# One attention tower on one core: row maxima cut and loaded in two halves, scores three slots later, a fill of one step less

## The chip, the cores and the metric

One Trainium2 chip; the kernel runs on one of its cores. The metric is the time of one execution on the device, in microseconds: before the change, the median of three runs is 1130.84 us (1127.64 to 1141.0). TensorE multiplies matrices into PSUM, VectorE (DVE), ScalarE (ACT) and GpSimd (POOL) compute, and SyncE (SP) issues nearly all DMA transfers, in the order of one list.

## The reference

For 32 sequences of 512 tokens and 128 channels: an embedding, an attention block of 8 heads of 16 channels, and a block of 4 experts, the last two with a residual and a layer norm. What matters here, in short:

```python
h = concat(pos[s], nest[nesting(ids)], seg[segments(ids)]) @ W
q, k, v = split(layernorm(h) @ qkv_w.T + qkv_b)          # 8 heads of 16
attn = softmax(q @ k.T / 4)                              # 512 x 512 per head
h = h + (attn @ v) @ out_w.T + out_b
h = h + experts(layernorm(h))                            # gate, relu(fc1), low rank, fc2
```

All of it is float32.

## The kernel before

Work is staged over sequences. A step t has 16 slots (c = 0 to 15), and in one step each stage works on another sequence: t+4 is embedded, t+3 gets its queries and keys scaled and cut into three bfloat16 pieces, whose stacks (`qstk`, `kstk`) go through DRAM, t+2 and t+1 get row maxima, t gets scores, exponentials and values, t-2 the projection, norm, gate and the first expert product, t-3 the rest. Steps run from -5 to 34, so the first ones fill the pipeline and the last ones empty it.

A head's 512 x 512 scores are made twice. First as 32 maximum tiles per sequence (128 queries x 512 keys, `scores`, L750), two in each slot, whose row maxima VectorE takes (`row_max`, L1025). From slot MSTART = 10 of a step the tiles are those of sequence t+2, before it those of t+1. When all 32 are in, `cut_max` (slot 10 of VectorE) splits the 32 negated maxima of each row into three bfloat16 parts with four chained instructions (L1033 to L1039), TensorE turns them (`turn_max`, L780, slot 11), ScalarE copies the turned rows (`copy_mT`, L610, slot 12), and SP loads them as 24 further rows of `qstk` (`load_max`, L379, "max_in"). Then the score tiles of the next step (`scores_T`, L724, two a slot from slot 0) come out with the maximum already taken off, and ScalarE only takes the exponential (L592). Values (L737) follow in blocks of eight products in slots 7, 11, 15 and 3.

Each engine runs its own written-out list: PE_ORDER and PRODUCTS say what TensorE does in a slot (BEFORE and BEHIND place a product around the values), ACT_WORK and DVE_WORK give (slot, place, name, sequence ahead, part), POOL_WORK and SP_WORK are the order of one step, and POOL_FILL and SP_FILL that of the fill. Maximum tiles and small products share four PSUM banks in turn (`mix`, three uses a slot), so a product may only start when the reader of the use four earlier is done (`mix_free`). Scores have a ring of three banks. Every wait is a semaphore count (`upto`), and an engine stops at it.

`hot` (L996) makes the one-hot of the token ids, `add_qk` (L1010) adds the position part to queries and keys, `finish` (L1104) adds the experts' product to the residual, `invert_den` (L1044) takes the reciprocal of the softmax denominators, and gate_first to gate_fourth (L1055 to L1092) are the chain of the gate. On POOL, `rstd_first` (L460) is a power, `residual`, `second` and `third` (L479, L485, L502) make the pieces, `normalise` (L528, L532) applies the denominators, `value` (L514, L520) writes the values.

## Time and profile before

| what | value |
|---|---|
| median of 3 runs | 1130.84 us (1127.64 to 1141.0) |
| profiled execution | 1126.86 us, its span 1125.1 us |
| TensorE busy | 1040.1 us (92%) |
| VectorE busy | 948.8 us (84%) |
| ScalarE busy | 807.0 us (72%) |
| POOL busy | 682.1 us (61%) |
| mean granted clock of TensorE | 0.962 |
| row maxima (L1025) | 1024 of 679 ns, 649.0 us |
| exponentials (L592) | 1024 of 600 ns, 556.3 us |
| DMA | 132.43 MB, mean 118 GB/s |

Busy times are read per engine from the profile's list. A mean duration of pipelined instructions is longer than the distance between two of them, so a row of several says more than a mean. The rows further down come from one execution; its steps are alike from the third on, and the one that begins at 859.87 us stands for them.

### The profile page before, as it was taken

The page shows a single profiled execution, that of the slowest core. Times are in us where ns is not written, and L with a number is a line of the kernel's source. Part 1 is how long each engine was busy: PE and PEld are TensorE (multiplying, and loading weights), DVE is VectorE, ACT ScalarE, POOL GpSimd, SP SyncE. Part 2 cuts the span into 40 slices and gives each one's busy share as a digit, 9 for nine tenths or more (in the row PEclk, how much of TensorE's full clock was granted, in tenths as well). Part 3 has the DMA queues.
Part 4 walks back from the last instruction along what each step waited for, and adds up shares of the span by engine and source line. Part 5 has one row for each costly group of instructions (what it writes and reads, how often), then busy time and mean ns, then how long its engine had stood idle before and what let it go on. Part 6 is the DMA issues. An engine that isn't in the chain of part 4 may idle for free.

```text
span 1125.1 us, 20263 instructions
## 1 busy us (share of the span) xinstructions
PE 1040.1 (92%) x6158; PEld 407.9 (36%) x6158; DVE 948.8 (84%) x2442; ACT 807.0 (72%) x1578; POOL 682.1 (61%) x684
## 2 busy tenths in 40 slices
PE   4368999999999999999999999999999999989865
PEld 2112233333434434343433443434343343333322
DVE  7498899999989989899999999999999998887312
ACT  2217787777877788787877778778787777856731
POOL 1855676677666666677666666667766666621231
PEclk9558999999999999999999999999999999999997
DMA  2553645555554445555555545565555554541111
GB/s 74 148 135 89 137 106 135 129 137 127 137 130 124 126 121 130 142 127 134 126 137 126 126 121 132 130 143 126 137 125 137 128 126 113 121 96 36 55 50 32
DMA packets 93530, 132.43 MB, mean 118 GB/s; under 512 B 18205, under 2 KB 69918, under 8 KB 87398
## 3 DMA queue, kind: packets, MB, share of 16 engines
q1 hardware_dynamic: 91872, 129.54, 47.9%
q10 hardware_dynamic: 1550, 1.59, 0.6%
q8 instruction: 50, 0.82, 0.3%
q14 instruction: 58, 0.48, 0.1%
HBM read 89.20 MB, written 35.01 MB: 110 GB/s over the span
## 4 chain that ended last, share of the span: by engine, by line
PE 64%; DVE 16%; DMA 6%; ACT 5%; issue 2%; POOL 1%; SPq 1%; POOLq 0%; ACTq 0%; DVEq 0%
PE pv L737 17%; PE mix L750 15%; PE sc L724 13%; DVE negmax L1025 9%; PE mix L804 7%; DMA den_dram<-ctx_sb 4%; PE mix L787 3%; DVE bn L1015 2%; ACT probs L592 2%; PE mix L809 2%; DVE h L1050 2%; PE mix L825 2%; DMA den<-den_dram 2%; ACT qk L596 1%; PE mix L769 1%
## 5 line engine op out<-in xcount | busy, mean ns | idle before, releaser
L1025 DVE TENSOR_REDUCE negmax<-mix 128x1 f32<-128x512 f32 x1024 | 649.0, 679 | 56.8 <-PE mix L750 56.2
L592 ACT ACTIVATE probs<-sc 128x512 f32<-128x512 f32 x1024 | 556.3, 600 | 118.2 <-PE sc L724 112.0
L724 PE MATMUL sc<-qstk,kstk 120*128 120x512 bf16 x1024 | 364.2, 382 | 5.6 <-ACT probs L592 4.9
L750 PE MATMUL mix<-kstk,qstk 96*128 96x512 bf16 x1024 | 331.7, 395 | 24.6 <-DMA kstk<-stack_dram 7.3
L737 PE MATMUL pv<-probs,vals 128*32 128x512 f32 x2048 | 244.8, 595 | 0.0
L528 POOL TENSOR_TENSOR ctxh<-ctx_sb,rdenb 128x512 f32<-128x512 f32 x64 | 81.0, 1268 | 245.3 <-DMA rdenb<-rden_dram 244.5
L750 PEld LDWEIGHTS mix<-kstk,qstk 96*128 96x128 bf16 x1024 | 89.4, 98 | 266.5 <-DVE negmax L1025 76.1
L724 PEld LDWEIGHTS sc<-qstk,kstk 120*128 120x128 bf16 x1024 | 100.1, 98 | 107.5 <-ACT probs L592 33.4
L804 PE MATMUL mix<-xn2T,fc1T_sb 128*128 128x512 f32 x256 | 138.2, 622 | 0.7 <-ACT hid L646 0.7
L508 POOL TENSOR_TENSOR qk<-qk,rstdb 128x512 f32<-128x512 f32 x64 | 81.1, 1269 | 57.9 <-DMA rstdb<-rstd_dram 53.4
L737 PEld LDWEIGHTS pv<-probs,vals 128*32 128x32 f32 x2048 | 59.1, 109 | 117.4 <-issue 100.1
L646 ACT ACTIVATE hid<-mix 128x512 f32<-128x512 f32 x128 | 76.5, 598 | 31.2 <-PE mix L804 28.7
L502 POOL TENSOR_TENSOR pieces<-qkr,pieces 128x512 bf16<-128x512 f32 x64 | 74.0, 1156 | 8.5
L485 POOL TENSOR_TENSOR pieces<-qk,pieces 128x512 bf16<-128x512 f32 x64 | 74.0, 1156 | 6.6 <-ACT pieces L600 6.6
L479 POOL TENSOR_TENSOR qkr<-qk,pieces 128x512 f32<-128x512 f32 x64 | 74.1, 1159 | 0.0
L460 POOL TENSOR_TENSOR rstd<-ve,minus_half 128x4 f32<-128x4 f32 x64 | 64.9, 1013 | 5.0
L458 POOL TENSOR_TENSOR ve<-mv,eps_sb 128x4 f32<-128x4 f32 x64 | 12.9, 201 | 73.8 <-DVE mv L1021 71.1
L804 PEld LDWEIGHTS mix<-xn2T,fc1T_sb 128*128 128x128 f32 x256 | 43.9, 191 | 36.7 <-DVE negmax L1025 24.7
L605 ACT COPY v<-mix 128x512 f32<-128x512 f32 x32 | 18.8, 586 | 46.8 <-POOL vals L520 39.1
L474 POOL TENSOR_TENSOR hb_sb<-h_sb,obias 128x512 f32<-128x512 f32 x32 | 40.5, 1265 | 15.0 <-DVE h L1050 14.8
L1010 DVE TENSOR_TENSOR qk<-mix,posQK 128x512 f32<-128x512 f32 x64 | 43.4, 679 | 7.1 <-POOL qkr L479 6.6
L1050 DVE TENSOR_TENSOR h<-mix,hb_sb 128x512 f32<-128x512 f32 x32 | 22.1, 692 | 28.6 <-PE mix L787 27.5
(141 smaller groups left out, 1088.5 us busy)
## 6 DMA issues: line engine op xcount, KB each, us to landing
stack_dram<-pieces SPq DMA_DIRECT2D x192, 128.0 KB
rdenb<-rden_dram SPq DMA_DIRECT2D x64, 256.0 KB
qstk<-stack_dram SPq DMA_DIRECT2D x31, 384.0 KB, 6.6
kstk<-stack_dram SPq DMA_DIRECT2D x31, 384.0 KB, 8.8
rstdb<-rstd_dram SPq DMA_DIRECT2D x32, 256.0 KB, 3.4
wrow<-w_dram SPq DMA_DIRECT2D x32, 256.0 KB
out<-out_sb SPq DMA_DIRECT2D x32, 256.0 KB, 2.6
qstk<-stack_dram SPq DMA_DIRECT2D x31, 256.0 KB, 7.0
```

The lines of the kernel that those rows point to most:

```text
L479: pool.tensor_tensor(qkr[:, side, :], qk32[:, side, :], pieces[:, side, 0, :], ALU.subtract).then_inc(s_res0, 1)
L485: pool.tensor_tensor(pieces[:, side, 1, :], qk32[:, side, :], pieces[:, side, 0, :], ALU.subtract).then_inc(s_pc1, 1)
L502: pool.tensor_tensor(pieces[:, side, 2, :], qkr[:, side, :], pieces[:, side, 1, :], ALU.subtract).then_inc(s_pc2, 1)
L508: pool.tensor_tensor(qk32[:, side, :], qk32[:, side, :], rstdb[:], ALU.mult).then_inc(s_scaled, 1)
L528: pool.tensor_tensor(ctxh[:, g, :], ctx_sb[:, u % 2, g, :], rdenb[:, g, :], ALU.mult).then_inc(s_ctxh, 1)
L592: act.activation(probs[:, c % 8, i % 2], sc[:, i % RING], ACT.Exp).then_inc(s_exp, 1)
L646: act.activation(hid[:, e, :], aux(f"fc1_{e}", 1), ACT.Relu).then_inc(s_hid, 1)
L724: pe.matmul(sc[:, i % RING, :], kstk[0:KROWS, u, h, j * P:(j + 1) * P], qstk[0:KROWS, u, h, :], start=True, stop=True).then_inc(s_score, 1)
L737: mm = pe.matmul(pv[Q * i:Q * i + Q, :], vals[:, u, 2 * half + jj, 4 * g + i, :], probs[:, 4 * (r % 2) + i, jj, :], start=(half == 0 and j ...
L750: pe.matmul(max_bank(m), qstk[0:STK, u, h, j * P:(j + 1) * P], kstk[0:STK, u, h, :], start=True, stop=True).then_inc(s_mxmm, 1)
L804: pe.matmul(aux(f"fc1_{e}", 1), fc1T_sb[:, e, :], xn2T[:], start=True, stop=True).then_inc(s_fc1mm, 1)
L1025: dve.tensor_reduce(negmax[:, m // NT, m % NT:m % NT + 1], max_bank(m), AX.X, ALU.max, negate=True).then_inc(s_max, 1)
```

## The change

The maxima are cut, turned, copied and loaded in two halves of four heads each. The maximum tiles of a sequence start at slot 7 of the step ahead of its own (MSTART 7) and end in slot 6 of its own; its scores start at slot 3 (SSTART) and end in slot 2 of the next step. The first half is cut in slot 15 and its load stands first in SP's list of the next step; the second is cut in slot 7, turned behind the values of that slot into the free part of the bank that holds the gates, and loaded behind `rden_out`. The stacks are loaded one step ahead, right behind the first half's load, and three buffers hold them instead of four. The embedding and all behind it stand one step nearer, so the steps run from -4. The one-hot gets two buffers and moves to slot 11, the product of v moves to slot 4, its copy to slot 5. The normalisation on POOL waits for the gate chain of the sequence before.

```diff
-KROWS = STK + 3 * NH
+MROWS = 3 * NH // 2
+KROWS = STK + MROWS
-MSTART = 10
+SSTART, MSTART = 3, 7
-U = 4
-HB, H2 = 5, 2
+U, UV = 3, 4
+HB, H2 = 4, 2
 PRODUCTS = [
-    ("project", -2), ("fc1_3", -3), ("embed", 4), ("low", -3), ("none", None), ("xn2T", -2), ("out", -3), ("gates", -2),
-    ("turn_gates", -2), ("fc1_0", -2), ("fc1_1", -2), ("mT", 1), ("q", 4), ("fc1_2", -2), ("k", 4), ("v", 4),
+    ("project", -2), ("fc1_3", -3), ("embed", 3), ("low", -3), ("v", 3), ("xn2T", -2), ("out", -3), ("gates", -2),
+    ("turn_gates", -2), ("fc1_0", -2), ("fc1_1", -2), ("turned", 3), ("q", 3), ("fc1_2", -2), ("k", 3), ("mT", 1),
 ]
-BEFORE, BEHIND = (3, 7), (11,)
+BEFORE, BEHIND = (3, 7), (11, 15)
 DVE_WORK = [
...
-    (6, 1, "moments1", 4, 0), (7, 1, "finish", -3, 0), (7, 1, "invert_den", -1, 0),
-    (9, 0, "gate", -2, 0), (10, 1, "gate", -2, 1), (10, 1, "gate", -2, 2), (10, 1, "gate", -2, 3),
-    (13, 0, "add_qk", 4, 0), (15, 1, "add_qk", 4, 1), (15, 1, "hot", 5, 0),
+    (6, 1, "moments1", 3, 0), (7, 1, "cut", 0, 1), (7, 1, "finish", -3, 0), (7, 1, "invert_den", -1, 0),
+    (9, 0, "gate", -2, 0), (10, 1, "gate", -2, 1), (10, 1, "gate", -2, 2), (10, 1, "gate", -2, 3), (11, 1, "hot", 4, 0),
+    (13, 0, "add_qk", 3, 0), (15, 1, "cut", 1, 0), (15, 1, "add_qk", 3, 1),
 ]
 SP_WORK = [
-    ("piece", 3, (0, 0)), ("piece", 3, (1, 0)), ("den_out", -1, 1), ("piece", 3, (0, 1)), ("den_in", -1, 0),
...
+    ("max_in", 0, 0), ("stack", 1, 0), ("stack", 1, 1),
+    ("piece", 2, (0, 0)), ("piece", 2, (1, 0)), ("den_out", -1, 1), ("piece", 2, (0, 1)), ("den_in", -1, 0),
+    ("piece", 2, (0, 2)), ("ids", 4, 0), ("out", -3, 0), ("piece", 2, (1, 1)), ("rden_out", -1, 0), ("max_in", 0, 1),
+    ("rden_in", -1, 0), ("piece", 2, (1, 2)), ("rstd_out", 3, 0), ("den_out", 0, 0), ("weights_out", -2, 0),
+    ("rstd_in", 3, 0), ("weights_in", -2, 0),
 ]
...
-            for t in range(-5, NSEQ + 3):
+            for t in range(-4, NSEQ + 3):
...
-            def load_max(b, u):
-                upto(sp, s_mT, b)
-                sp.dma_start(qstk[STK:KROWS, u, :, :],
-                             mT[:].unsqueeze(1).broadcast_to([3 * NH, NH, S])).then_inc(s_mrow, 16)
+            def load_max(b, g, u):
+                upto(sp, s_mT, b, 8, 4 * g + 4)
+                sp.dma_start(qstk[STK:KROWS, u, 4 * g:4 * g + 4, :],
+                             mT[:, g].unsqueeze(1).broadcast_to([MROWS, 4, S])).then_inc(s_mrow[g], 16)
...
-            def normalise(b, u):
-
+            def normalise(b):
+
+                if b < NSEQ - 1:
+                    upto(pool, s_gate, b - 1, 13)
...
+            def copy_mT(b, g):
+
+                upto(act, s_mTmm, b, 2, g + 1)
+                upto(act, s_mrow[g], b - 1, 16)
+                bank = aux(("mT", "gates")[g], 1)
+                for j in range(NT):
+                    act.copy(mT[:, g, j * P:(j + 1) * P], bank[Q * j:Q * j + MROWS, g * P:g * P + P]).then_inc(s_mT, 1)
...
-                if i == 0:
-                    upto(pe, s_mrow, b, 16)
+                if i % 16 == 0:
+                    upto(pe, s_mrow[g], b, 16)
...
+            def turn_max(b, g):
+
+                upto(pe, s_mp, b, 8, 4 * g + 4)
+                bank = aux(("mT", "gates")[g], 1)
                 for j in range(NT):
+                    mm = pe.matmul(bank[Q * j:Q * j + MROWS, g * P:g * P + P], mpc[:, g, j].rearrange("p a h -> p (a h)"),
+                                   id16[:], start=True, stop=True)
                 mm.then_inc(s_mTmm, 1)
...
+            def second_half(t):
+
+                if runs(t - 2):
+                    upto(pe, s_gat, t - 2)
+                else:
+                    mix_free(t, 3 * 7 + 1)
+                turn_max(t, 1)
...
+            def cut_max(b, g):
+
+                nm, res = (x.rearrange("p h j -> p j h") for x in (negmax[:, 4 * g:4 * g + 4], mres[:]))
+                n = 4 * g
+                upto(dve, s_max, b, 32, 16 * g + 16)
+                upto(dve, s_mTmm, b - 1, 2, g + 1)
+                dve.tensor_copy(mpc[:, g, :, 0, :], nm).then_inc(s_mp, 1)
+                upto(dve, s_mp, b, 8, n + 1)
+                dve.tensor_tensor(res, nm, mpc[:, g, :, 0, :], ALU.subtract).then_inc(s_mp, 1)
+                upto(dve, s_mp, b, 8, n + 2)
+                dve.tensor_copy(mpc[:, g, :, 1, :], res).then_inc(s_mp, 1)
+                upto(dve, s_mp, b, 8, n + 3)
+                dve.tensor_tensor(mpc[:, g, :, 2, :], res, mpc[:, g, :, 1, :], ALU.subtract).then_inc(s_mp, 1)
```

VectorE's list of one steady step, before, from the end of slot 6 to slot 10 (`negmax` are the row maxima, `mpc` the cut parts, `out_sb` the output addition, `rden` the reciprocal, `lmax` and `lsub` the first part of the gate):

```order
L1021 BN_AGGR mv<-bn 128x2 x4
L1025 TENSOR_REDUCE negmax<-mix 128x1 x2
L1104 TENSOR_TENSOR out_sb<-mix,h 128x512
L1044 RECIPROCAL rden<-den 128x32
L1025 TENSOR_REDUCE negmax<-mix 128x1 x3
L1055 TENSOR_REDUCE lmax<-mix 128x4
L1057 TENSOR_SCALAR lsub<-mix 128x4
L1060 TENSOR_TENSOR lsub<-mix,lmax 128x4x4
L1025 TENSOR_REDUCE negmax<-mix 128x1 x2
L1033 CAST mpc<-negmax 128x4x8
L1035 TENSOR_TENSOR mres<-negmax,mpc 128x32
L1037 CAST mpc<-mres 128x4x8
```

The same place now:

```order
L1042 BN_AGGR mv<-bn 128x2 x4
L1046 TENSOR_REDUCE negmax<-mix 128x1 x2
L1055 CAST mpc<-negmax 128x4x4
L1057 TENSOR_TENSOR mres<-negmax,mpc 128x4x4
L1059 CAST mpc<-mres 128x4x4
L1061 TENSOR_TENSOR mpc<-mres,mpc 128x4x4
L1126 TENSOR_TENSOR out_sb<-mix,h 128x512
L1066 RECIPROCAL rden<-den 128x32
L1046 TENSOR_REDUCE negmax<-mix 128x1 x3
L1077 TENSOR_REDUCE lmax<-mix 128x4
L1079 TENSOR_SCALAR lsub<-mix 128x4
L1082 TENSOR_TENSOR lsub<-mix,lmax 128x4x4
```

The cut of one half stands ahead of the output addition in slot 7, and none stands in slot 10.

SP's list of one steady step, before, around the load of the maxima (`qstk<-mT`) and the loads of the stacks:

```order
L369 DMA den_dram<-ctx_sb 4x512 [waits s_denin,s_ctx]
L379 DMA qstk<-mT 24x8x512 [waits s_mT]
L375 DMA w_dram<-turned 4x4x128 [waits s_win,s_wT]
L412 DMA rstdb<-rstd_dram 128x512 [waits s_rstdout,s_scaled]
L417 DMA wrow<-w_dram 128x1x512 [waits s_wout,s_low]
L356 DMA qstk<-stack_dram 48x1x4096 [waits s_score,s_pcoutq]
```

The same place now:

```order
L370 DMA den_dram<-ctx_sb 4x512 [waits s_denin,s_ctx]
L376 DMA w_dram<-turned 4x4x128 [waits s_win,s_wT]
L413 DMA rstdb<-rstd_dram 128x512 [waits s_rstdout,s_scaled]
L418 DMA wrow<-w_dram 128x1x512 [waits s_wout,s_low]
L380 DMA qstk<-mT 12x4x512 [waits s_mT]
L357 DMA qstk<-stack_dram 48x1x4096 [waits s_score,s_pcoutq]
```

The stack loads stand behind a load of half the maxima, which waits for ScalarE's copy in slot 0 of the new step.

## Rows read from the trace of the kernel before

**Rows 1.** Busy times by stretch: front, step 1, a steady step, the tail.

```profile
core 0: us, PE busy (x) PEld busy (x) DVE busy (x) ACT busy (x) POOL busy (x), PEclk, DMA share, GB/s
49.09:85.16 36.07, 26.06 (x70) 6.14 (x70) 33.81 (x64) 5.26 (x10) 24.19 (x25) 0.50 0.61 142
113.02:139.70 26.68, 24.47 (x149) 7.66 (x146) 23.87 (x50) 20.89 (x40) 18.01 (x17) 1.00 0.60 133
859.87:891.05 31.18, 31.04 (x192) 12.35 (x191) 28.69 (x75) 24.91 (x49) 21.25 (x21) 1.00 0.55 131
984.90:1020.20 35.30, 32.31 (x188) 12.67 (x181) 28.70 (x62) 22.00 (x43) 7.10 (x7) 0.95 0.37 84
1020.20:1076.50 56.30, 51.74 (x312) 20.13 (x310) 25.82 (x77) 41.79 (x85) 14.21 (x14) 1.00 0.14 44
```

**Rows 2.** Timeline of VectorE, slots 7 to 15: start, duration, what, idle before.

```profile
873.09 1.26 DVE L1025 TENSOR_REDUCE negmax<-mix 128x1 f32<-128x512 f32 x2
874.26 0.68 DVE L1104 TENSOR_TENSOR out_sb<-mix,h 128x512 f32<-128x512 f32 x1
875.51 0.35 DVE L1044 RECIPROCAL rden<-den 128x32 f32<-128x32 f32 x1 [0.57 <-DMA den<-den_dram]
876.01 1.89 DVE L1025 TENSOR_REDUCE negmax<-mix 128x1 f32<-128x512 f32 x3
...
879.67 0.19 DVE L1033 CAST mpc<-negmax 128x32 bf16<-128x32 f32 x1
...
880.35 0.19 DVE L1039 TENSOR_TENSOR mpc<-mres,mpc 128x32 bf16<-128x32 f32 x1
...
886.50 3.07 DVE L1025 TENSOR_REDUCE negmax<-mix 128x1 f32<-128x512 f32 x5
889.49 0.68 DVE L1010 TENSOR_TENSOR qk<-mix,posQK 128x512 f32<-128x512 f32 x1
890.09 0.34 DVE L996 TENSOR_SCALAR onehot<-ids_b,const_sb 96x512 bf16<-96x512 bf16 x1
891.25 0.69 DVE L1025 TENSOR_REDUCE negmax<-mix 128x1 f32<-128x512 f32 x1 [0.83 <-PE mix L750]
```

**Rows 3.** Timeline of POOL in the same step.

```profile
873.63 1.01 POOL L460 TENSOR_TENSOR rstd<-ve,minus_half 128x4 f32<-128x4 f32 x1
874.60 1.17 POOL L479 TENSOR_TENSOR qkr<-qk,pieces 128x512 f32<-128x512 f32 x1
875.90 1.15 POOL L502 TENSOR_TENSOR pieces<-qkr,pieces 128x512 bf16<-128x512 f32 x1
883.55 1.26 POOL L528 TENSOR_TENSOR ctxh<-ctx_sb,rdenb 128x512 f32<-128x512 f32 x1 [6.50 <-DMA rdenb<-rden_dram]
```

**Rows 4.** Timeline of VectorE in the front: the first cut.

```profile
73.73 0.95 DVE L1033 CAST mpc<-negmax 128x32 bf16<-128x32 f32 x1
74.72 0.21 DVE L1035 TENSOR_TENSOR mres<-negmax,mpc 128x32 f32<-128x32 f32 x1
74.96 0.46 DVE L1037 CAST mpc<-mres 128x32 bf16<-128x32 f32 x1
75.45 0.55 DVE L1039 TENSOR_TENSOR mpc<-mres,mpc 128x32 bf16<-128x32 f32 x1
```

**Rows 5.** Timeline of POOL at the same time.

```profile
73.38 1.26 POOL L514 TENSOR_TENSOR v<-v,posV 128x512 f32<-128x512 f32 x1
74.72 1.23 POOL L520 TENSOR_TENSOR vals<-v,rstd 128x256 f32<-128x256 f32 x2
```

**Rows 6.** Timeline of SP: the issues of the stack loads.

```profile
859.11 1.97 SPq L356 DMA_DIRECT2D qstk<-stack_dram  x3
861.18 1.58 SPq L363 DMA_DIRECT2D kstk<-stack_dram  x3
```

**Rows 7.** DMA issues by form: KB of one, median us to landing.

```profile
kstk<-stack_dram SPq DMA_DIRECT2D x33, 128.0 KB, 10.4
```

**Rows 8.** Timeline of TensorE: last tile of slot 6, first of slot 7.

```profile
872.55 0.60 PE L750 MATMUL mix<-kstk,qstk 96*128 96x512 bf16 x2
```

**Rows 9.** One line of ScalarE, the copy of turned weights: ns min/median/max.

```profile
L636 ACT COPY turned<-mix x32: 257/257/258, 163.2 to 1111.9; 16x128 f32<-16x128 f32 x32
```

More of the change, by code:

```diff
@@ L81 @@
-    ("residual", 3, 1), ("third", 3, 1), ("normalise", -1, 0), ("v", 3, 0),
+    ("scale", 2, 0), ("add_bias", 2, 0), ("scale", 2, 1), ("rstd2", -2, 0), ("norm2", -2, 0),
+    ("second", 2, 0), ("residual", 2, 0), ("third", 2, 0), ("second", 2, 1), ("rstd1", 3, 0),
+    ("residual", 2, 1), ("third", 2, 1), ("normalise", -1, 0), ("v", 3, 0),
 ]
 SP_WORK = [
-    ("piece", 3, (0, 0)), ("piece", 3, (1, 0)), ("den_out", -1, 1), ("piece", 3, (0, 1)), ("den_in", -1, 0),
-    ("piece", 3, (0, 2)), ("ids", 5, 0), ("out", -3, 0), ("piece", 3, (1, 1)), ("rden_out", -1, 0), ("piece", 3, (1, 2)),
@@ L95 @@
 ]
 POOL_FILL = [
-    ("add_bias", 3, 0), ("scale", 3, 0), ("scale", 3, 1), ("rstd1", 4, 0),
-    ("second", 3, 0), ("residual", 3, 0), ("third", 3, 0), ("second", 3, 1), ("residual", 3, 1), ("third", 3, 1), ("v", 3, 0),
+    ("add_bias", 2, 0), ("scale", 2, 0), ("scale", 2, 1), ("rstd1", 3, 0),
+    ("second", 2, 0), ("residual", 2, 0), ("third", 2, 0), ("second", 2, 1), ("residual", 2, 1), ("third", 2, 1), ("v", 3, 0),
 ]
@@ L270, in tower @@
         s_mp = sem("s_mp")
-        s_mTmm, s_mT, s_mrow = sem("s_mTmm"), sem("s_mT"), sem("s_mrow")
+        s_mTmm, s_mT = sem("s_mTmm"), sem("s_mT")
+        s_mrow = [sem(f"s_mrow{g}") for g in range(2)]
         s_score, s_exp, s_pv, s_ctx = sem("s_score"), sem("s_exp"), sem("s_pv"), sem("s_ctx")
@@ L451, in _ @@
         def _(pool):
-            for v in range(U):
+            for v in range(UV):
                 pool.memset(vals[:, v, :, 0:4, HC:Q], 1.0).then_inc(s_pconst, 1)
@@ L662, in step @@
                 for c in range(SLOTS):
-                    if t == -4 and c == 13:
+                    if t == -3 and c == 13:
                         fill_heads()
+                    if t == -3 and c == 4:
+                        copy_rT(0)
                     for place in range(3):
                         for name, ahead, part in [w[2:] for w in ACT_WORK if w[:2] == (c, place)]:
-                            if runs(t + ahead):
+                            if runs(t + ahead) and not (name == "rT" and t == -3):
                                 work[name](t + ahead, (u + ahead) % U, part)
-                        if place < 2 and runs(t):
-                            exp(t, 2 * c + place)
+                        b = t if c >= SSTART else t - 1
+                        if place < 2 and runs(b):
+                            exp(b, 2 * ((c - SSTART) % SLOTS) + place)
             steps(act, step)
@@ L889, in product @@
                     products[name][0](t + ahead)
+            def second_half(t):
[4 more added lines that the diff above has]
+                turn_max(t, 1)
             def step(t, u):
                 for c in range(SLOTS):
-                    if t == -4 and c == 3:
+                    if t == -3 and c == 3:
                         fold_positions()
-                    if t == -4 and c == 8:
+                    if t == -3 and c == 4:
                         product(t, 11)
                     for what, i in PE_ORDER:
-                        if (what == "before" and c in BEFORE or what == "behind" and c in BEHIND) and t > -4:
+                        if (what == "before" and c in BEFORE or what == "behind" and c in BEHIND) and (t, c) != (-3, 11):
                             product(t, c)
-                        if what == "scores" and runs(t):
-                            scores_T(t, 2 * c + i, u)
+                        if what == "behind" and c == 7 and runs(t):
+                            second_half(t)
+                        if what == "scores":
+                            b, v = (t, u) if c >= SSTART else (t - 1, (u - 1) % U)
+                            if runs(b):
+                                scores_T(b, 2 * ((c - SSTART) % SLOTS) + i, v)
                         if what == "max":
@@ L1112, in _ @@
                 "hot": lambda b, u, _: hot(b),
+                "cut": lambda b, u, g: cut_max(b, g),
                 "add_pos": lambda b, u, _: add_pos(b),
```

145 lines of the change are left out of this document (58 added, 87 removed).

## The prediction

> **What bounds the kernel now.** I read the stretches first, then the instructions of one step in order of time, then two places of the front. A step is one pass of 16 slots; the one that begins at 859.87 us (slot 0) stands for all from the third on. In its 31.18 us TensorE shows 31.04 us busy and VectorE 28.69 [rows 1]. VectorE's own rows leave hardly more: its idle time before a row is 0.57 us in slot 7 (waiting for the denominators' transfer) and 0.83 after slot 15 [rows 2]. So two engines run almost without a gap and hold each other: TensorE may be only four PSUM banks ahead of VectorE, and the next bank comes free when VectorE has read it. The front is different: from the first maximum tile (49.09) to the first score tile (85.16) it takes 36.07 us, at a granted clock of 0.50, the lower of the two levels (1.2 GHz) [rows 1]. The sum below is made against the profiled execution, 1126.86 us, which is 4.0 us under the median of the runs, 1130.84.
>
> **The front.** Slots decide what must be done before the first score: before, 12 tiles of the first sequence, its other 20, 12 of the second and one more, 45; now 18, 6 and one, 25. At the stretch's own pace 20/45 of 36.07 us goes: -16. From the other side, 20 maxima at 0.61 us (five in 3.07 [rows 2]) are 12. I take 16, since the additions between the maxima go with them. Steps 0 and 1 give some back. The stacks are now loaded one step ahead instead of three, and land about 14.7 us after slot 0 (worked out below). Slot 7 begins after 12.9/31.18 of a step, which in step 1 (26.68 us [rows 1]) is 11.0 us: about 3.5 us late there and as much in step 0, which in turn holds six scores fewer (about 0.4 us each at the low clock, an estimate from the 0.22 below, doubled): together +4.
>
> **The tail.** The last 26 maxima move into the two steps before the last scores, which take 56.30 us with VectorE busy 25.82 and TensorE 51.74 [rows 1]: a tile takes 0.22 us of TensorE (an estimate: two in a row show 0.60, overlapping [rows 8]), so they need 5.7, and 4.6 are free; I take +3. Three slots of scores behind the last step: six exponentials, +2 after overlap. The step from 984.90 takes 35.30 us, some 4 more than the steady one [rows 1]; the new wait of the normalisation on the gate chain should take away most of it: -3. Together +2.
>
> **The steady step, edit by edit.**
> - The cut of the maxima (four chained VectorE instructions, 879.67 to 880.54, 0.87 us [rows 2]) leaves slot 10: -0.87. Two cuts of the same four come instead. Half the elements save almost nothing, so each is 0.87 where it runs free.
> - The cut in slot 7 doesn't run free. It starts when the maximum of slot 7 ends, 874.35, and at that time POOL works without a gap: power 873.63 to 874.64, residual to 875.77, third piece to 877.05; then it is idle for 6.50 us, which is where the old cut stood [rows 2, 3]. What that does is shown in the front, where the old cut met POOL: first instruction 0.95 us instead of 0.19, the third 0.46, the fourth 0.55 instead of 0.19, each ending as a POOL instruction ends (73.38 + 1.26 = 74.64; two `vals` of 0.62 to 75.34 and 75.95), and the second passing in 0.21: 73.73 to 76.00, 2.27 us [rows 4, 5]. By that pattern the slot-7 cut waits for the power (874.64), passes, waits for the residual (875.77) and for the third piece: it ends at about 877.1. Behind it in VectorE's order stand the output addition (0.68) and the reciprocal (0.35; its input has landed by 875.51): 878.1, where the next maximum before started at 876.01 [rows 2]: +2.1. TensorE waits for it twice, at the half's turn and at the bank of slot 6, which the output addition must read.
> - The one-hot (0.34 [rows 2]) moves from slot 15, where idle time followed it, to slot 11, where five maxima run back to back: +0.34.
> - Slot 15: before, 889.57 to 891.25 from one maximum to the next, with 0.83 idle [rows 2]. Now a cut (0.87), the addition (0.68) and the bank that TensorE may use only after it (about 0.24): 1.8, +0.1. POOL's `v` and `vals` end about there; taken as free.
> - Sum: -0.87 + 2.1 + 0.34 + 0.1 = +1.7 us a step.
> - Taken at nothing: four more turns on TensorE (0.2 us, within the wait above); eight copies of a quarter row instead of one on ScalarE, which is busy 24.91 of 31.18 us [rows 1]; half the bytes of the maxima's load. The second half's load stands behind `rden_out` on SP and has three slots, 3/16 of the step or 5.8 us, until slot 11 needs it; I take it as just in time, and up to 1 us a step of delay stays in the range. Each block of values now needs the exponentials of the slot just before it; slot 7's first tile, two scores and the gate product lie between, and where they don't cover it, it costs at most one exponential (0.6 us) a block.
> - The stack loads move from 0.76 us ahead of slot 0 (859.11) to behind the half's load. That waits for the turn, for four copies of 0.26 us [rows 9] and for its own issue; with the turn ending about when slot 15's last tile starts, the stacks' first issue stands about 1.2 us after slot 0. SP's six issues span 859.11 to 862.76 [rows 6]; the last lands 10.4 us after its start [rows 7], 12.7 after slot 0 before and 14.7 now. TensorE's first maximum of slot 7 stood at 872.76 [rows 8], 12.9 after slot 0, and 13.2 with the product `v` now ahead of it. So it may be 1.5 us late. But VectorE's cut behind it then starts at 875.9 and still ends just after the third piece. Most of this wait lies beside the other one; I price it as a rival.
>
> **The sum.** 1126.9 - 16 + 4 + 2 + 28 steps x 1.7 (48) = 1165 for an execution like the profiled one, and with the 4.0 us up to the median 1169.
>
> The Trainium skill, in "SBUF — State Buffer", section "Who interferes with whom", says that casts in a two-port mode and instructions with two SBUF inputs share a port pair with GpSimd, that the later one waits for the whole instruction of the other, and that issue order alone decides. It agrees with three of the four rows of the front; the second instruction, which has two SBUF inputs, passed because POOL's was not yet issued. If every instruction of the cut lost that race, the cut would end about 0.8 us later and the sum would be 22 us more.
>
> **Rivals.**
> 1. *Both waits in full* (chance 0.18). The loads are late by all of 1.5 us, the cut starts at 875.9, meets the third piece with its first instruction and needs its 0.87 after 877.05: 877.9, +0.8 a step: 28 x 2.5 = 70, 1191. For it: a load of the same size issued later lands later. Against it: the load of the maxima, which stood just ahead of the stacks, has half the bytes.
> 2. *The cuts find POOL's gaps* (0.27), the one that ends not slower. Place: slot 7. If the cut ends before the residual does, or POOL's small instructions do not hold it up, it costs 0.87, the output addition follows at 875.3 and the next maximum at 876.3, +0.25; the step changes by -0.87 + 0.25 + 0.34 + 0.1 = -0.2, and TensorE, full already, makes that 0: 1126.9 - 10 + 4 = 1121. It decides from a step gain of +0.9 downwards: 28 x 0.9 - 10 + 4 is within 2% of the median. For it: the new cut stands just where VectorE was idle for 0.57 us. Against it: POOL's row is without a gap there.
> 3. *The idle spots are filled* (0.10). As 2, and the 0.57 and 0.83 us of idle time are used up by the two cuts, so that slot 10's 0.87 is gained nearly whole: -0.6 a step, 1104.
> The forecast has 0.45, between 1150 and 1180 (step gains of 1.2 to 2.1).
>
> **Chances and range.** What a measurement of this kernel can tell from no change I take as 2%, about 23 us: faster is below 1108, slower above 1153. The forecast with rival 1 gives slower, less a tenth for its lower edge: 0.54. Rival 2 and that edge: 0.35. Rival 3, and a little of rival 2: 0.11. For 8 in 10 the range goes from 1112 (rival 2 with a slightly shorter step) to 1188 (most of rival 1).
>
> **What would show it.** In the changed kernel's profile: the first score near 69 us instead of 85.16; the steady step at 32.5 to 33.3 us; in slot 7 the casts of the cut at 0.5 to 1.2 us mean instead of 0.19, and TensorE's turn waiting for them; the wait of the maxima for `kstk` in every step if rival 1 holds. It is wrong if those casts show 0.19 us, or if the step stays at 31.2.

## The result, and the profile after

The changed kernel takes 1199.36 us (median of four executions, 1193.44 to 1202.39) against 1129.24 before: a ratio of 1.060, 95% interval 1.051 to 1.069. It is slower, as forecast, but by 66.6 us between the two profiled executions (1193.4 against 1126.9) where the sum said 38. The profiled execution is the fastest of its four; between the medians it is 70 us. The time lies above the range.

Places of both traces can be laid over each other: slot 0 of a step (the pair of maximum tiles at its start) and the output additions, the first in slot 7 of step 3. The first score stands in slot 0 before and in slot 3 now.

| place | before, us | after, us | difference there |
|---|---|---|---|
| first score | 85.16 | 71.50 | -13.7 |
| slot 0 of step 0 | 84.33 | 67.06 | -17.3 |
| slot 0 of step 1 | 113.02 | 101.01 | -12.0 |
| slot 0 of step 2 | 139.70 | 133.70 | -6.0 |
| first output addition | 184.83 | 182.28 | -2.6 |
| the 27th | 999.83 | 1065.43 | +65.6 |
| the last | 1121.65 | 1188.23 | +66.6 |

From the first to the 27th output addition there are 26 steps: 31.35 us each before, 33.97 after, +2.62. That is nearly everything. The front gained about what was forecast and most of it was given back before the first output.

Busy times by stretch in the changed kernel, as in [rows 1]: the front from the first maximum to the first score, steps 0 and 1, and a steady step.

```profile
52.69:71.50 18.81, 14.27 (x37) 3.18 (x38) 17.25 (x31) 1.29 (x5) 12.08 (x13) 0.50 0.33 86
67.06:101.01 33.95, 29.22 (x126) 8.16 (x127) 28.04 (x53) 19.41 (x42) 14.73 (x15) 0.73 0.38 85
101.01:133.70 32.69, 26.41 (x149) 8.45 (x149) 27.14 (x54) 23.14 (x49) 16.74 (x16) 0.95 0.46 105
913.86:947.98 34.12, 31.76 (x195) 12.57 (x195) 32.11 (x79) 26.43 (x57) 21.84 (x22) 1.00 0.50 117
```

TensorE's busy time in a steady step has hardly grown (31.76 against 31.04), but 2.4 us of idle time stand beside it. VectorE is busy for 32.11 instead of 28.69. Two cuts of 0.82 in place of one of 0.87 would be 0.8 of that; the rest is instructions that have become longer (in this step also the one-hot, 1.37 instead of 0.34).

VectorE's timeline shows which (start, duration, what, idle time before): first the cut of slot 15, then that of slot 7, as in [rows 2].

```profile
911.48 0.43 DVE L1055 CAST mpc<-negmax 128x16 bf16<-128x16 f32 x1
911.95 0.19 DVE L1057 TENSOR_TENSOR mres<-negmax,mpc 128x16 f32<-128x16 f32 x1
912.17 0.46 DVE L1059 CAST mpc<-mres 128x16 bf16<-128x16 f32 x1
912.66 0.54 DVE L1061 TENSOR_TENSOR mpc<-mres,mpc 128x16 bf16<-128x16 f32 x1
913.12 0.68 DVE L1031 TENSOR_TENSOR qk<-mix,posQK 128x512 f32<-128x512 f32 x1
...
928.68 0.16 DVE L1055 CAST mpc<-negmax 128x16 bf16<-128x16 f32 x1
928.88 0.19 DVE L1057 TENSOR_TENSOR mres<-negmax,mpc 128x16 f32<-128x16 f32 x1
929.10 1.11 DVE L1059 CAST mpc<-mres 128x16 bf16<-128x16 f32 x1
930.24 0.18 DVE L1061 TENSOR_TENSOR mpc<-mres,mpc 128x16 bf16<-128x16 f32 x1
930.34 0.68 DVE L1126 TENSOR_TENSOR out_sb<-mix,h 128x512 f32<-128x512 f32 x1
```

POOL at the same two places, as in [rows 3] (L509 scales the queries of the next step):

```profile
910.58 1.30 POOL L515 TENSOR_TENSOR v<-v,posV 128x512 f32<-128x512 f32 x1
911.96 1.21 POOL L521 TENSOR_TENSOR vals<-v,rstd 128x256 f32<-128x256 f32 x2
913.13 1.26 POOL L509 TENSOR_TENSOR qk<-qk,rstdb 128x512 f32<-128x512 f32 x1
...
928.04 1.01 POOL L461 TENSOR_TENSOR rstd<-ve,minus_half 128x4 f32<-128x4 f32 x1
929.02 1.16 POOL L480 TENSOR_TENSOR qkr<-qk,pieces 128x512 f32<-128x512 f32 x1
```

Read the ends. In slot 15 the first cast ends with `v` (911.88), the second with the first half of `vals`, the last subtraction with the other (913.17). In slot 7 the second cast starts 0.08 us behind the residual and ends with it (930.2). The cast and the subtraction ahead of it pass in 0.16 and 0.19 beside the power. In the slot 15 that follows, it is the scaling behind the `vals` that holds the cut's second instruction to its own end (946.86):

```profile
945.75 1.15 DVE L1057 TENSOR_TENSOR mres<-negmax,mpc 128x16 f32<-128x16 f32 x1
```

```profile
945.54 1.32 POOL L509 TENSOR_TENSOR qk<-qk,rstdb 128x512 f32<-128x512 f32 x1
```

TensorE at both places: its turn of the half (L793) waits for the cut, and the next maximum for the addition behind the cut.

```profile
913.35 0.23 PE L793 MATMUL mix<-id,mpc 128*12 128x128 bf16 x4 [0.71 <-DVE mpc L1061]
913.86 0.60 PE L759 MATMUL mix<-kstk,qstk 96*128 96x512 bf16 x2 [0.28 <-DVE qk L1031]
...
930.57 0.23 PE L793 MATMUL mix<-id,mpc 128*12 128x128 bf16 x4 [0.26 <-DVE mpc L1061]
931.08 0.60 PE L759 MATMUL mix<-kstk,qstk 96*128 96x512 bf16 x2 [0.28 <-DVE out_sb L1126]
```

All 64 cuts of the run give a simple law. From the end of a slot-15 cut to the start of the next slot-7 cut there are 15.48 us in nearly every steady step, and from the end of that one to the next slot-15 cut 14.34. So a step is 29.82 us plus its two cuts, and what a cut lasts above 0.82 us is in the step one to one. The slot-7 cut lasts 1.74 in all steady steps but one (1.77 on average). The slot-15 cut lasts between 1.2 and 2.6 in the 26 steps, 2.12 on average (2.05, as the first expectation has it, where the cut of step 2, 0.80, is counted and the last is not). It meets a row of four POOL instructions, now at one link and now at another: `v` in 5 of the 26 steps, the two `vals` in 25, and the scaling behind them in 17. If each link's excess is put down to the POOL instruction with which it ends, 15 of the 34 us that this cut loses in the 26 steps go to the `vals` and 17 to the scaling.

29.82 + 1.77 + 2.12 are 33.7 of the 33.97. Most of what is left (0.2 a step) are three steps whose stretch of 15.48 is 17.1. It isn't `kstk` that is late there, as two of the expectations have it: TensorE's waits for it are 0.7 us in all from 300 to 1000 us, and none lies in these stretches. In each of the three the granted clock stands at 0.50 for 3.4 us, after TensorE had waited 1.3 to 1.6 us for the cut (one of these waits is the first row, and the stretch behind it the second; the others begin at 675.87 and 812.41):

```profile
302.08 0.23 PE L793 MATMUL mix<-id,mpc 128*12 128x128 bf16 x4 [1.58 <-DVE mpc L1061]
```

```profile
303.82:307.23 3.41, 3.41 (x11) 1.88 (x10) 2.85 (x7) 1.46 (x3) 1.67 (x2) 0.50 0.51 111
```

SP's stack loads and their landing, as in [rows 6, 7] (the last row is of the list of DMA issues: KB of one, median us to landing):

```profile
914.75 0.83 SPq L380 DMA_DIRECT2D qstk<-mT  x1
915.68 1.87 SPq L357 DMA_DIRECT2D qstk<-stack_dram  x3
917.65 1.58 SPq L364 DMA_DIRECT2D kstk<-stack_dram  x3
```

```profile
kstk<-stack_dram SPq DMA_DIRECT2D x33, 128.0 KB, 8.4
```

They are issued 1.8 us after slot 0, where the forecast had 1.2, and land in 8.4 us, not in the 10.4 of before.

### The profile page after: what moved, and what is told of

It is laid out like the page before. It is cut to its first block, busy times and chain, and to the rows that moved or that the text cites. A ratio compares the mean times of both kernels' runs of the same rounds, so it can differ in the third digit from the quotient of the medians.

```text
span 1191.6 us, 21091 instructions
## 1 busy us (share of the span) xinstructions
PE 1054.4 (88%) x6286; PEld 420.8 (35%) x6286; DVE 1027.7 (86%) x2570; ACT 851.8 (71%) x1802; POOL 682.3 (57%) x684
## 4 chain that ended last, share of the span: by engine, by line
PE 42%; DVE 39%; issue 6%; ACT 4%; DMA 4%; POOL 2%; SPq 1%; POOLq 0%; ACTq 0%; DVEq 0%
DVE negmax L1046 21%; PE mix L759 11%; PE pv L746 10%; PE sc L733 8%; PE mix L817 5%; DVE mpc L1059 4%; DVE qk L1031 3%; PE mix L800 3%; DVE bn L1036 3%; PE mix L822 2%; ACT probs L595 2%; DVE mres L1057 2%; DVE out_sb L1126 2%; DVE h L1072 2%; DMA kstk<-stack_dram 1%
## 5 line engine op out<-in xcount | busy, mean ns | idle before, releaser
L733 PE MATMUL sc<-qstk,kstk 108*128 108x512 bf16 x1024 | 370.3, 385 | 3.3 <-ACT probs L595 1.7
L759 PE MATMUL mix<-kstk,qstk 96*128 96x512 bf16 x1024 | 325.3, 391 | 41.5 <-DVE qk L1031 11.3
L759 PEld LDWEIGHTS mix<-kstk,qstk 96*128 96x128 bf16 x1024 | 85.1, 98 | 234.1 <-DVE negmax L1046 61.9
L616 ACT CAST mT<-mix 12x128 bf16<-12x128 f32 x256 | 65.9, 258 | 137.7 <-PE mix L793 133.0
L733 PEld LDWEIGHTS sc<-qstk,kstk 108*128 108x128 bf16 x1024 | 99.7, 98 | 119.0 <-ACT probs L595 39.1
L509 POOL TENSOR_TENSOR qk<-qk,rstdb 128x512 f32<-128x512 f32 x64 | 81.0, 1267 | 21.3 <-DMA rstdb<-rstd_dram 20.0
L793 PE MATMUL mix<-id,mpc 128*12 128x128 bf16 x256 | 15.0, 222 | 46.6 <-DVE mpc L1061 46.3
L1059 DVE CAST mpc<-mres 128x16 bf16<-128x16 f32 x64 | 51.1, 799 | 2.2
```

The costliest lines, as they stand in the source:

```text
L509: pool.tensor_tensor(qk32[:, side, :], qk32[:, side, :], rstdb[:], ALU.mult).then_inc(s_scaled, 1)
L733: pe.matmul(sc[:, i % RING, :], kstk[0:KROWS, u, h, j * P:(j + 1) * P], qstk[0:KROWS, u, h, :], start=True, stop=True).then_inc(s_score, 1)
L759: pe.matmul(max_bank(m), qstk[0:STK, u, h, j * P:(j + 1) * P], kstk[0:STK, u, h, :], start=True, stop=True).then_inc(s_mxmm, 1)
L1059: dve.tensor_copy(mpc[:, g, :, 1, :], res).then_inc(s_mp, 1)
```

## The experiments

Each ratio is to the kernel before the change, measured beside it, with its 95% interval. "Step" is the mean of the 26 steps of its profiled execution. Each diff is against the changed kernel or the one named.

| kernel | median, us | ratio | step, us |
|---|---|---|---|
| before | 1129.24 | 1 | 31.35 |
| changed | 1199.36 | 1.060 (1.051 to 1.069) | 33.97 |
| values first | 1172.95 | 1.038 (1.034 to 1.043) | 33.24 |
| cut early | 1182.34 | 1.048 (1.045 to 1.052) | 33.50 |
| both | 1149.67 | 1.020 (1.017 to 1.023) | 32.32 |
| stacks first | 1384.76 | 1.228 (1.223 to 1.233) | 40.74 |
| reciprocal later | 1153.5 | 1.023 (1.020 to 1.027) | 32.33 |
| one-hot in slot 15 | 1157.77 | 1.026 (1.023 to 1.029) | 32.52 |
| nine unread products | 1159.64 | 1.028 (1.025 to 1.030) | 32.54 |
| second half's load first | 1134.2 | 1.006 (1.004 to 1.009) | 31.89 |
| addition first | 1135.19 | 1.006 (1.004 to 1.008) | 31.71 |
| more unread products | 1133.64 | 1.005 (1.003 to 1.007) | 31.78 |
| keys' stack first | 1295.12 | 1.148 (1.145 to 1.150) | 37.84 |
| the same, fill as it was | 1294.24 | 1.147 (1.145 to 1.149) | 37.51 |

### POOL out of the way of the slot-15 cut

```diff
-    ("residual", 2, 1), ("third", 2, 1), ("normalise", -1, 0), ("v", 3, 0),
+    ("residual", 2, 1), ("third", 2, 1), ("v", 3, 0), ("normalise", -1, 0),
```

> The changed kernel with one edit on POOL: the product of v and its two `vals` stand ahead of the normalisation instead of behind it, in the 7.65 us in which POOL waits for `rdenb`. Theory (the cuts are held up by POOL's two-input instructions): in the changed kernel the cut in slot 15 lasts 2.05 us on average in the steady steps (0.80 to 2.6) and the time from its end to the cut in slot 7 is the same 15.48 us in nearly all of them; with POOL out of its way it lasts 0.82, the step goes from 33.9 to 32.7, and the time falls by 28 x 1.23 = 34 us, to about 1165. Rival A (what bounds the step is the finer chain behind the cut: turn, four copies, the half's load, the stack loads): the casts get shorter, the time falls by less than 10 us, to about 1190. Rival B (the normalisation, now up to 2.5 us later, is the next thing late): the casts get shorter, and TensorE waits for `ctxn` at slot 0 instead: no change or slower, 1199.

Measured: the slot-15 cut lasts 0.82 in 21 of the 26 steps (1.00 on average), the step is 0.72 shorter and the time 26 us. The scaling now starts behind the cut in these 21, and meets it in the other five. Neither rival: the chain behind the cut did not hold the time, nor did the normalisation. Less came than expected for two reasons of 0.25 us a step each: the slot-7 cut, still 1.74 in most steps, met more than one POOL instruction in four (3.4 to 3.7 us there, 2.01 on average), and the stretch behind it grew, where TensorE now waits for `kstk` (3.7 us in 8 waits from 300 to 1000 us).

### The slot-7 cut 0.6 us earlier

```diff
-    (7, 1, "cut", 0, 1), (7, 1, "finish", -3, 0), (7, 1, "invert_den", -1, 0),
+    (7, 0, "cut", 0, 1), (7, 1, "finish", -3, 0), (7, 1, "invert_den", -1, 0),
```

> The changed kernel with one edit on VectorE: the cut of slot 7 stands ahead of that slot's first maximum, 0.6 us earlier, where POOL runs only its power and no residual. Theory: in the changed kernel that cut lasts 1.74 us in every steady step, all of it above 0.82 in one cast that ends with POOL's residual, while the two instructions that run beside the power pass in 0.16 and 0.19; ahead of the maximum all four are done before the residual starts: 0.82, and the time falls by 28 x 0.92 = 26 us, to about 1173. Rival A (the power blocks as I had it): the first instruction now waits for the power's end, and the cut stays near 1.2 to 1.8: a fall of 0 to 15 us. Rival B (finer chain): the casts get shorter and the time does not.

Measured: the cut lasts 0.82 in every steady step but the last, though all of it runs beside POOL's power, so the power holds up nothing. The step is 0.47 shorter and the time 17 us, half of what the casts lost. The other half came back as a wait of VectorE for `den`, which the changed kernel doesn't have (8.8 us in 11 waits from 300 to 1000 us).

### Both edits

> The changed kernel with the edits of the first two together. Theory: the steady step is 15.48 + 14.34 + 2 x 0.82 = 31.5 us, what it was before the change (31.3), and the time falls by 28 x 2.15 = 60 us, to about 1139; if the three late loads of `kstk` (1.6 us each) grow in number with the shorter step, up to 1160. Rival A (finer chain): 1185 or more. Rival C (the two edits share their gain): less than the sum of their gains by more than 15 us.

Measured: 0.82 and 0.93 for the cuts, 1149.67 us, 50 of the 60 us expected and more than the two gains together (26 and 17). The same cast over all 64 cuts (min/median/max in ns), in the changed kernel and then here, each from that kernel's own answer on this line:

```profile
L1059 DVE CAST mpc<-mres x64: 174/1106/1245, 65.1 to 1127.3; 128x16 bf16<-128x16 f32 x64
```

```profile
L1059 DVE CAST mpc<-mres x64: 174/175/1280, 65.1 to 1082.6; 128x16 bf16<-128x16 f32 x64
```

The step is 32.32, not 31.5. From the slot-7 cut to the next slot-15 cut it is 14.94 at best but up to 16.7. Of the waits of VectorE from 300 to 1000 us (what waited, for what: us in total, times, longest) one is not there in the changed kernel:

```profile
DVE rden L1066 <- DMA den<-den_dram: 9.0, 11, 1.6
```

### The stack loads ahead of the half's load

```diff
-    ("max_in", 0, 0), ("stack", 1, 0), ("stack", 1, 1),
+    ("stack", 1, 0), ("stack", 1, 1), ("max_in", 0, 0),
```

> The changed kernel with SP's list of a step beginning with the six stack loads, and the load of the first half of the maxima behind them; SP is idle for 4 us there, so they are issued about 3.5 us earlier and the half's load hardly later. Theory: the stack loads are late in three steady steps only, by 1.6 us each, so the gain is 5 us at most (1194), or nothing or a loss of up to 1.5 us a step (1240) where the half's load, now behind 2.3 MB of transfers, lands after slot 3. Rival A (the late stack loads are a main part of the 2.6 us a step): 20 us or more faster.

Measured: 185 us slower. SP's issues in one step, and TensorE's first score behind them:

```profile
898.12 1.89 SPq L357 DMA_DIRECT2D qstk<-stack_dram  x3
900.11 1.59 SPq L364 DMA_DIRECT2D kstk<-stack_dram  x3
903.19 0.89 SPq L380 DMA_DIRECT2D qstk<-mT  x1
```

```profile
911.62 1.04 PE L733 MATMUL sc<-qstk,kstk 108*128 108x512 bf16 x2 [3.84 <-DMA qstk<-mT]
```

The half's 48 KB arrive 8.4 us after their issue, behind 1.5 MB. In the changed kernel, issued at 914.75 ahead of the stacks, they were there when the scores of slot 3 began at 919.15. My bound of 1.5 us a step was far too low (6.8 us came): TensorE waits 3.84 us in this row, and the granted clock stands at 0.50 for 6.8 us from shortly before the end of that wait on (910.70 to 917.53; 1.00 in the 12.6 us ahead).

Whether late stack loads are a main part of the loss, this run can't tell: `kstk` is no wait here, but the wait for the half covers everything. The changed kernel's own trace says no (0.7 us in three waits, above).

### The reciprocal one slot later

Against the kernel with both edits:

```diff
-    (7, 1, "invert_den", -1, 0),
+    (8, 1, "invert_den", -1, 0),
```

> The kernel with both cuts free, with one more edit on VectorE: the reciprocal of the denominators stands behind the second maximum of slot 8 instead of slot 7, three instructions of 0.6 us later. Theory (scores three slots later make the denominators three slots later, and an earlier arrival at the reciprocal only turns into a wait): in the kernel with both cuts free VectorE waits for `den` in 11 of 21 steps, 9.0 us in all, 0.43 us a step; these go, and the time falls by 28 x 0.43 = 12 us, to about 1138. Rival D (the normalisation is late next, since POOL's wait for `rdenb` begins with this reciprocal; or the half's load, queued behind the store of the reciprocals): no change, 1150, and TensorE waits for `qstk` at slot 11 longer than the 2.4 us in 21 steps that it waits now. Rival E (TensorE is full anyway: 31.4 us a step by its own work): 1150.

Measured: no gain (1153.5). VectorE's wait for `den` is gone, and TensorE waits at slot 11 for the second half's load, in every step:

```profile
PE sc L733 <- DMA qstk<-mT: 12.6, 22, 1.1
```

Rival D was right: on SP that load stood behind the store of the reciprocals. The wait had only changed its engine.

### The one-hot back in slot 15

Against the kernel before it, in steady steps only:

```diff
-    (15, 1, "cut", 1, 0), (15, 1, "add_qk", 3, 1),
+    (15, 1, "cut", 1, 0), (15, 1, "add_qk", 3, 1), (15, 1, "hot", 4, 0),
```

> The same with the one-hot of the steady steps back behind slot 15's addition (in the fill it stays in slot 11). Theory: in slot 11 it costs its 0.34 us in full and 1.37 where it meets POOL's normalisation (0.15 us a step on average); in slot 15 VectorE stands idle for 0.48 us behind the addition. A step is 0.3 to 0.5 us shorter, the time 8 to 14 us: about 1127, level with the kernel before the change or just under it. Rival E (TensorE's own work sets the step): no change. Rival F (it delays the bank that TensorE waits for, the idle time being TensorE's answer to the addition and not slack): half of it or nothing.

Measured: 1157.77, nothing gained. The wait of slot 11 hides what slot 11 might have given, so this alone doesn't tell Rival E from F; but the stretch from the slot-15 cut to the next cut became 0.25 us longer (15.27 instead of 15.02 in the median step), as Rival F has it.

### Unread products in the fill

Against the kernel before it:

```diff
+WARM = {(-2, 11): 2, (-1, 2): 2, (-1, 7): 5}
...
+            def warm(n):
+                for _ in range(n):
+                    pe.matmul(pv[:], id32[:], posT_sb, start=True, stop=True)
...
+                    warm(WARM.get((t, c), 0))
```

> The same with nine float32 matrix products added on TensorE in three places of the fill where it sits idle for 5, 5 and 10 us (their result goes to a bank that is not in use and is read by nobody). Theory for the front: after the change step 0 runs 19 us at a granted clock of 0.50, before it 7 us; with TensorE busy in the idle stretches the clock comes back before step 0, which becomes 4 to 8 us shorter, and so does the time: about 1120. Rival G (step 0 is bound by the loads, the copies and VectorE, not by the clock): the clock is higher and the time the same within 2 us. Rival H (the products delay the first maxima): 3 us longer or more. Rival I: the granted clock does not answer to them: no change.

Measured: 1159.64, no change (in the profiled execution the first maximum comes 0.4 us earlier than in the kernel before it and the first output 4.4 later; why stays open). The granted clock answered and then fell again in the gap of 5.45 us that the products left before the first maximum:

```profile
42.00:48.00 6.00, 4.68 (x16) 1.94 (x13) 0.00 (x0) 0.35 (x1) 4.18 (x6) 1.00 0.63 168
48.00:54.00 6.00, 1.87 (x4) 0.44 (x4) 3.16 (x13) 2.92 (x5) 5.87 (x6) 0.68 0.81 201
```

So it didn't try the question; a later run does.

### The second half's load ahead of the store

Against the kernel with the reciprocal in slot 8 (the one-hot in slot 11):

```diff
-    ("piece", 2, (1, 1)), ("rden_out", -1, 0), ("max_in", 0, 1),
+    ("piece", 2, (1, 1)), ("max_in", 0, 1), ("rden_out", -1, 0),
```

> The kernel with both cuts free and the reciprocal in slot 8, with one more edit on SP: the load of the second half of the maxima stands ahead of the store of the reciprocals. Theory: in the run before, the wait for `den` was gone from VectorE and had come back one to one on TensorE, which waited for that half's load at slot 11 in each of 22 steps, 12.6 us in all (0.57 us a step), because the store that stands ahead of it on SP waits for the reciprocal. Ahead of the store the load is issued about 1 us earlier; the wait goes, the steady step falls from 32.3 to 31.7 us and the time by 28 x 0.57 = 16 us, to about 1137. Rival D (the normalisation is late next, its reciprocals being stored 0.9 us later): half of that or nothing, with TensorE waiting at slot 0 for `ctxn`. Rival E (TensorE is full: 32.3 us is its own work): no change.

Measured: 1134.2, 19 us faster. The first output stands at 176.0 (182.28 in the changed kernel). VectorE's cut of slot 7, free, and POOL's residual that now begins when it is over:

```profile
875.13 0.18 DVE L1055 CAST mpc<-negmax 128x16 bf16<-128x16 f32 x1
875.34 0.19 DVE L1057 TENSOR_TENSOR mres<-negmax,mpc 128x16 f32<-128x16 f32 x1
875.56 0.17 DVE L1059 CAST mpc<-mres 128x16 bf16<-128x16 f32 x1
875.77 0.18 DVE L1061 TENSOR_TENSOR mpc<-mres,mpc 128x16 bf16<-128x16 f32 x1
```

```profile
875.95 1.16 POOL L480 TENSOR_TENSOR qkr<-qk,pieces 128x512 f32<-128x512 f32 x1
```

What TensorE still waits for from 300 to 1000 us:

```profile
PE mix L759 <- DVE qk L1031: 6.2, 22, 0.3
PE mix L759 <- DMA kstk<-stack_dram: 2.7, 9, 0.5
```

Whether the load's place alone would do, with the reciprocal left in slot 7, was not tried.

### The addition ahead of slot 15's first maximum

Against the kernel just above:

```diff
-    (15, 1, "cut", 1, 0), (15, 1, "add_qk", 3, 1),
+    (15, 0, "add_qk", 3, 1), (15, 0, "cut", 1, 0),
```

> The same with the addition to the keys and the cut of slot 15 ahead of that slot's first maximum, in this order. Theory: TensorE waits 0.28 us for that addition in every step (5.8 us in 21), since its bank is the one that the slot's second maximum needs; 0.6 us earlier the wait goes, and the time falls by 28 x 0.28 = 8 us, to about 1129. Rival F (TensorE then waits for the slot's first maximum, or for the cut): no change within 4 us. Rival G (the cut, which keeps its place in time, now meets POOL): 10 us or more slower.

Measured: 1135.19, the same as without it. The wait for the addition is gone, the step is 0.18 shorter, and the stack loads are late in its place:

```profile
PE mix L759 <- DMA kstk<-stack_dram: 7.7, 15, 0.8
```

The first output stands 5.6 us later than in the run before; the cut met POOL in the first steps (1.82, 3.91 and 1.20 us, where it was 0.81, 2.82 and 0.82), which is 2.5 of the 5.6.

### More unread products

Against the kernel just above, halves of 256 columns: `WARM = {(-2, 11): 7, (-1, 2): 8, (-1, 7): 20}`, one in each slot from 8 of step -1 to 2 of step 0.

> The same with more unread products on TensorE in the fill (two float32 quarters at a time, 0.45 us at the full clock: 7, 8 and 20 in the three idle stretches, one in each slot from the first maximum on to slot 2 of step 0). With nine products the granted clock rose to 1.00 between 42 and 48 us and fell back to 0.50 in the gap of 5.45 us that they left before the first maximum. Theory: with the gap closed and the slots filled the clock stays up through step 0, TensorE, busy for 18.4 of the 20 us from 70 to 90 us at 0.50 before, needs half as long for it, and the time falls by 4 to 8 us against the run without them. Rival G (step 0 is bound by the loads and VectorE): less than 2 us. Rival H (the added products delay the maxima): 2 us slower or more.

Measured: 1133.64, 1.5 us under it, inside both intervals. From 66 to 90 us, without and with them:

```profile
66.00:90.00 24.00, 20.46 (x78) 5.79 (x80) 17.37 (x38) 13.87 (x30) 12.12 (x13) 0.66 0.51 107
```

```profile
66.00:90.00 24.00, 18.60 (x92) 6.76 (x92) 17.91 (x40) 14.25 (x31) 12.42 (x13) 0.86 0.51 108
```

The clock is 0.86 instead of 0.66 and the first output comes 2.1 us earlier. Rival G: this rise of the clock hardly shortens step 0. The 0.50 that the changed kernel has there was not tried.

### The keys' stack ahead of the half's load

Against the kernel with the addition first; the second run also keeps the addition and the cut in their old place up to step 2.

```diff
-    ("max_in", 0, 0), ("stack", 1, 0), ("stack", 1, 1),
+    ("stack", 1, 1), ("max_in", 0, 0), ("stack", 1, 0),
```

> The last kernel without the added products, with SP's list of a step beginning with the three loads of the keys' stack, then the load of the first half of the maxima, then the three loads of the queries' stack. Theory: with both cuts free and the step at 31.7 us, TensorE waits for the stack loads in 15 of 22 steps, 7.7 us in all (0.35 us a step): the rival of the prediction that shows only when the step is short again. With half of the 1.5 MB ahead of the half's load, where SP is idle, the last of them lands about 3 us earlier, and the half's load, which lands late by 4 us behind all six, lands just in time behind three: 28 x 0.35 = 10 us faster, about 1125. Rival A (the half's load lands after slot 3): slower by 1 us a step or more, 1165. Rival E (TensorE is full at 31.7 us): no change.

> The same, but up to step 2 the addition and the cut of slot 15 keep their place behind the first maximum. Theory: ahead of it the cut met POOL in the fill (1.82, 3.91 and 1.20 us in its first three steps, 0.81, 2.82 and 0.81 behind it), and the first output stands 5.6 us later (181.56 against 176.0); this comes back: 5 us faster than the run without it, about 1120. Rival (the 5.6 us come from elsewhere, such as the loads): no change within 2 us.

Measured: 1295.12 and 1294.24. Rival A: TensorE waits for the half's load again, though only three loads stand ahead (the row is of the first of the two runs).

```profile
PE sc L733 <- DMA qstk<-mT: 82.4, 19, 6.2
```

Issued at 919.22 in one step, the load let the scores go on at 928.1, 8.9 us later. The trace shows why. The last of the three loads ahead of it, issued at 917.20, landed 10.7 us later, at 927.89, and the scores went on 0.2 us behind that; in all 28 waits of this kind in the run it is 0.2 to 0.6 us. Meanwhile the queries' loads, issued behind the half's, were moved as well: two of the three landed before that load did (926.9 and 927.8).

The second run is inconclusive, since that wait covers the fill. No kernel here beats the one before the change; the best come to 1.005 and 1.006 of it.

## Why the prediction failed

**The front, -16: nearly right.** From the first maximum to the first score it takes 18.81 us instead of 36.07, -17.3, and slot 0 of step 0 comes 17.3 earlier. But the first maximum stands 3.6 us later (52.69 instead of 49.09), which the sum didn't have, so the first score came at 71.50 and not near 69: -13.7.

**Steps 0 and 1, +4: too small.** They take 5.3 and 6.0 us more. I charged late stack loads, and TensorE's wait for `kstk` in step 0 is 0.52 us. The cuts of this stretch last 2.49, 2.87, 1.76 and 2.34 us. From slot 0 of step 0 to the first output 14.7 us were given back where I had 6.4 (4 here and 1.7 a step from there); with the cuts and the second half's load mended the first output is 6.3 us earlier. The lower clock, for 19 us of step 0 instead of 7, seems a small part of it: raised from 0.66 to 0.86 it gave 2.1 us at the first output. What the other 8.4 consist of I leave open.

**The cut in slot 7: the mechanism was right, the size was not.** It meets POOL where I said and TensorE waits for it. But it is held up once, by the residual, not by the power and the third piece as well: 1.74 us instead of 2.75. From "values first" to "both" it is worth 0.92 us a step, not 2.1.

The Trainium skill's "SBUF — State Buffer", section "Who interferes with whom", has POOL keep the shared ports for the whole of an instruction that it issued first. The residual, the `vals` and the scaling agree (1.11 us for a cast of 0.17, 1.15 for a subtraction of 0.19). The power doesn't: it ran from 928.04 to 929.05 while a cast passed in 0.16 and a subtraction with two SBUF inputs in 0.19.

**The step that failed: slot 15, "POOL's `v` and `vals` end about there; taken as free", +0.1.** They don't end there. The cut meets the `vals` in 25 of the 26 steps, and in 17 it is then caught by the scaling behind them, which the prediction doesn't name: 2.12 us instead of 0.87. Freeing it gave 0.72 us a step from the changed kernel and 1.18 with the slot-7 cut already free, 26 and 33 us of time. I had looked at POOL's rows for slot 7 and not for slot 15. They were in the trace of before: the `vals` ran to 890.10, across the 889.57 where the sum put the cut.

```profile
887.57 1.27 POOL L514 TENSOR_TENSOR v<-v,posV 128x512 f32<-128x512 f32 x1
888.92 1.18 POOL L520 TENSOR_TENSOR vals<-v,rstd 128x256 f32<-128x256 f32 x2
891.50 1.27 POOL L508 TENSOR_TENSOR qk<-qk,rstdb 128x512 f32<-128x512 f32 x1 [1.40 <-DMA rstdb<-rstd_dram]
```

The scaling waited for its load there and began 1.9 us after that place; in the rows of the changed kernel it follows the `vals` without a wait.

**-0.87 for slot 10 and +0.34 for the one-hot: neither shows.** With both cuts free the shortest steps are 31.6 us, and 31.25 where the addition of slot 15 stands first as well, against 31.2 before. That agrees with a full TensorE (31.04 of 31.18 us in [rows 1]): what VectorE gains or loses below TensorE's own time then counts nothing. It is argued and not shown, since no run takes work off TensorE. I had used that sentence for a rival and not for the sum.

**The second half's load "just in time": right**, and near the edge: TensorE's waits for it, 0.3 us in all from 300 to 1000 us, are 2.4 with the cuts free and 12.6 with the reciprocal a slot later.

**The stack loads, 1.5 us late: wrong.** They land 2 us sooner than before, and TensorE waits for them three times from 300 to 1000 us, 0.3 us at most. Rival 1 has the nearest time (1191), for a reason that the trace refutes: its late loads don't show, and its slot-7 cut is shorter than the forecast's. Late stack loads do come at a step of 31.7 us (7.7 us in 22 steps).

**The tail, +2: right** (+1.0). The step with the gate chain is 3.4 us shorter (34.78 to 31.38), as the wait on the gate was to make it; no run tries that wait alone.

**The sum.** Of 28.6 us that are missing, 24 lie in steps 2 to 29, 7 in steps 0 and 1; the front and the tail give back 2. Steps 2 to 29 are 72 us longer than before. The two cuts' meetings with POOL are shown to be 46 of these (50 of the time), and behind them the denominators, the store and the second half's load in one chain 12 (15 to 19 of the time, with what it gives in the fill). In the kernel with the addition first a step is still 0.36 us over that of before, and TensorE's wait for the stack loads is 0.35 a step. Of the signs named, the casts of slot 7 are as forecast (0.16 and 1.11, 0.64 on average), and the step, 33.97, lies above the 32.5 to 33.3.

## What to carry to other kernels

When a chain of short VectorE instructions moves, lay POOL's timeline under every new place, to the tenth of a microsecond, and ask which long two-input instruction is issued just before each link, and which comes behind that one if the link is late. Moving the cut by 0.6 us in one slot, and POOL's instructions to another place of their list for the other, was enough here. A wait that vanishes from one engine has not been won until the next list (here SP's) is read: what stands behind the moved instruction inherits it. A small urgent load belongs ahead of the large ones in its queue: half-way among them cost 160 us here, behind them 185.

## What the hardware showed that I had not expected

- A power of 4 elements a partition on POOL (1.01 us) holds up neither a cast nor a two-input subtraction on VectorE (0.16 and 0.19 us beside it); a two-input instruction of 512 elements holds up the same cast to its end (1.11). A chain of four short links can be held at one link after another: 1.2 to 2.6 us for 0.82.
- A load of 48 KB behind 1.5 MB on SP's queue took 8.4 us from issue to its reader, and 8.9 behind 0.77 MB with as much issued right after it; ahead of them less than 4.4. The Trainium skill's "DMA: Bandwidth & Descriptors", section "Queues, rings and completion order", has each transfer engine take a ring's descriptors in order, which agrees with both: the reader went on 0.3 and 0.2 us after the last load issued ahead had landed. In the second the 0.77 MB ahead aren't alone in these 8.9 us: 640 KB issued behind the half landed before the last of them did. How much sooner the half would land without what follows, no run here shows.
- The granted clock stood at 1.00 from 42 to 48 us with unread products on TensorE, where it had been 0.50 without them, and fell back in a stretch where TensorE was idle for 5.45 us. In the steady steps of the changed kernel it fell to 0.50 three times, for 3.4 us each, after waits of 1.3 to 1.6 us; each such step is 1.6 us longer. Other waits of that length left it at 1.00.
